# Attention in a decoder layer: denominators from products with ones, transposed heads side by side in one bank, their copies on ScalarE

## What is computed

```python
q = (x @ Wq).reshape(B, T, H, Dh)      # B=4, T=512, H=16, Dh=32; k and v likewise
scores = jnp.einsum('bthd,bshd->bhts', q, k)
scores = scores * jnp.tril(jnp.ones((T, T)))
attn = jax.nn.softmax(scores / T ** 0.5, axis=-1)
out = jnp.einsum('bhts,bshd->bthd', attn, v).reshape(B, T, H * Dh)
return out @ Wo
```

## Time and profile before

| | us |
|---|---|
| median of 3 runs (lowest, highest) | 1652.87 (1651.56, 1653.89) |
| profiled execution: span, first to last instruction | 1654.5 |
| PE / DVE / ACT / Pool busy in the span | 1527.9 / 1068.2 / 709.6 / 123.1 |
| attention loops, as read here | 90-161, 238-310, 389-461, 537-605 |

### The profile page before, as it was taken

How to read it: one execution, slowest core, us unless ns; L and a number is a source line. 1 busy time by engine, 2 the same in 40 slices (tenths; PEclk the granted TensorE clock), 3 DMA queues, 4 the chain that set the end, 5 groups by cost and what they waited for, 6 DMA issues and landing times.

```text
span 1654.5 us, 29864 instructions
## 1 busy us (share of the span) xinstructions
PE 1527.9 (92%) x9280; PEld 769.2 (46%) x9280; DVE 1068.2 (65%) x2408; ACT 709.6 (43%) x1578; POOL 123.1 (7%) x189
## 2 busy tenths in 40 slices
PE   5877987997799788989999999999999999999998
PEld 3455445545554554434444444444444444444443
DVE  6488568567955976666666666666666666666444
ACT  4378158526923862333333333333333333333332
POOL 1512002100300351000000000000000000000000
PEclk8999989998999999999999999999999999999999
DMA  6641432142125230211111111111111111111111
GB/s 191 160 144 51 121 91 72 53 127 89 59 78 149 84 97 23 80 40 67 53 40 65 54 40 64 55 40 61 58 40 58 60 40 57 62 40 42 59 51 51
DMA packets 73553, 118.41 MB, mean 72 GB/s; under 512 B 10096, under 2 KB 54384, under 8 KB 68848
## 3 DMA queue, kind: packets, MB, share of 16 engines
q1 hardware_dynamic: 73456, 117.20, 22.4%
HBM read 93.32 MB, written 23.86 MB: 71 GB/s over the span
## 4 chain that ended last, share of the span: by engine, by line
PE 78%; DVE 10%; issue 5%; SPq 2%; ACT 2%; DMA 2%; DVEq 0%; ACTq 0%
PE bank L538 23%; PE bank L539 23%; PE bank L540 23%; DVE bank L1144 3%; PE bank L595 3%; PE bank L614 2%; PE bank L551 1%; PE bank L584 1%; DVE mx L1144 1%; DMA qk_dram<-qk 1%; DVE w_split L1345 1%; PE bank L623 1%; DVE prob_t L1158 1%; PE bank L668 1%; PE bank L654 1%
## 5 line engine op out<-in xcount | busy, mean ns | idle before, releaser
L538 PE MATMUL bank<-xf,ring 128*128 128x512 f16 x1024 | 388.2, 379 | 0.0
L540 PE MATMUL bank<-xf,ring 128*128 128x512 f16 x1024 | 388.2, 379 | 0.0
L539 PE MATMUL bank<-xf,ring 128*128 128x512 f16 x1024 | 388.2, 379 | 0.0
L538 PE MATMUL bank<-ring,hid 128*128 (+1 forms) x512 | 195.5, 382 | 9.5 <-DVE hid L1277 6.4
L539 PE MATMUL bank<-ring,hid 128*128 (+1 forms) x512 | 195.6, 382 | 0.0
L540 PE MATMUL bank<-ring,hid 128*128 (+1 forms) x512 | 195.3, 381 | 0.0
L1270 DVE SCALAR_TENSOR_TENSOR cube<-sq,g_sb 128x512 f32<-128x512 f32 x128 | 88.4, 690 | 144.5 <-ACT sq L967 144.2
L1144 DVE CUSTOM_DVE_ANT_0 bank<-bank,mask,col 128x128 f32<-128x128 f32 (+3 forms) x256 | 142.3, 556 | 36.9 <-PE bank L584 23.2
L595 PE MATMUL bank<-ident,prob 128*128 128x128 f32 x640 | 121.4, 297 | 46.0 <-DVE prob_t L1158 39.3
L973 ACT CAST hid<-inter 128x512 f16<-128x512 f32 x128 | 79.0, 618 | 197.7 <-DVE inter L1275 197.7
L964 ACT ACTIVATE g_sb<-bank,col 128x512 f32<-128x512 f32 x128 | 87.7, 685 | 172.0 <-PE bank L540 172.0
(11 more groups left out here) (144 smaller groups left out, 2120.6 us busy)
## 6 DMA issues: line engine op xcount, KB each, us to landing
xf<-xf_dram SPq DMA_DIRECT2D x32, 1024.0 KB, 4.9
stack<-qk_dram SPq DMA_DIRECT2D x128, 128.0 KB, 3.2
sc_in<-scale_t SPq DMA_DIRECT2D x32, 384.0 KB
qk_dram<-qk SPq DMA_DIRECT2D x32, 256.0 KB, 3.1
packed_t<-pk_t SPq DMA_DIRECT2D x32, 192.0 KB, 2.0
pk_in<-packed_t SPq DMA_DIRECT2D x32, 192.0 KB
X<-in_x_dram SPq DMA_DIRECT2D x4, 1024.0 KB, 6.6
pk_in<-L_ffn_gate_W_packed_dram SPq DMA_DIRECT2D x16, 256.0 KB, 3.0
```

The costliest lines, as they stand in the source:

```text
L538: pe.matmul(o, lhs(0), rhs(0), start=first, stop=False)
L539: pe.matmul(o, lhs(0), rhs(1), start=False, stop=False)
L540: return pe.matmul(o, lhs(1), rhs(0), start=False, stop=stop)
```

## The change

On PE `values` first forms the denominators: for each block and head a product of `ones_col` (128 x 32 of ones) with prob_t into columns 256 and up of bank 6, and for i < 3 one more of `e_count` with the identity. `recips` is gone, and with it its slot and ACT's copy. Pool makes e_count = (512 - wide) e_zero. DVE's `divide` becomes a reciprocal of 128 x 128 from the bank, a wait for it, and the multiplication; it stands at j = 1 of unit u+3 (`AT_DIVIDE` 13). DVE's `turned`, `all_tokens` and `reciprocals` are gone, and ACT's `exp` has no accumulator. The transposes of several heads share a slot (`PACKED`: 4 heads at i = 0, 2 at i = 1, 1 else), and ACT copies each slot once. `repack` goes from j = 1 to j = 3, behind values; its copies move to i = 1, j = 1 on ACT and to i = 2, j = 0 on DVE.

```diff
-        def turn_slot(h):
-            return h + 2 * (max(0, h - 2) // 16) + max(0, h // 4 - 1)
+        PACKED = [TT // (i + 1) if i < 2 else 1 for i in range(TT)]
+        order = []
+        for u in range(UNITS):
+            for j in range(4):
+                if j % PACKED[u % TT] == 0:
+                    order.append(("heads", u, j // PACKED[u % TT]))
+                if j == 3 and u % TT == 0 and u > 0:
+                    order += [("pack", u // TT - 1, 0), ("pack", u // TT - 1, 1)]
+        order += [("pack", HG - 1, 0), ("pack", HG - 1, 1)]
...
-        AT_RECIP, AT_DIVIDE = 9, 12
-        AT_SUMS, AT_TURNED, AT_RECIPROCALS = 1, 3, 2
+        AT_DIVIDE = 13
...
+                nc.gpsimd.tensor_scalar(e_count[:, u % 2, :], e_zero[:, u % 2, :], float(T - wide[i]), None, ALU.mult).then_inc(e_count_done, 1)
...
             def values(n, u):
-                pe.wait_ge(pt_act, n * 3 * UNITS + 3 * u + 3)
-                pe.wait_ge(pt_dve, n * UNITS + u + 1)
+                pe.wait_ge(pt_out, n * TURNED + groups_till(u + 1))
                 if u >= 1:
                     pe.wait_ge(o_done, n * UNITS + u)
...
+                for k in range(blocks):
+                    for j in range(4):
+                        mm = pe.matmul(bank[6][32 * j:32 * j + 32, 256 + at:256 + at + P], ones_col[:], prob_t[:, u % 2, j, P * k:P * k + P],
+                                       start=(k == 0), stop=(k == blocks - 1 and i == TT - 1))
+                if i < TT - 1:
+                    pe.wait_ge(e_count_done, beyond_units(n, u))
+                    for j in range(4):
+                        mm = pe.matmul(bank[6][32 * j:32 * j + 32, 256 + at:256 + at + P], e_count[:, u % 2, j:j + 1].to_broadcast([P, DH]), ident[:],
+                                       start=False, stop=True)
...
                         if j == 3 and u > 0:
-                            recips(n, u - 1)
                             values(n, u - 1)
-                        if j == 1 and u % TT == 0 and u > 0:
+                        if j == 3 and u % TT == 0 and u > 0:
                             repack(n, u // TT - 1)
...
-                                     bias=nmx[:, u % 2, j:j + 1], accum_out=den[:, u % 2, j:j + 1]).then_inc(exp_done, 1)
+                                     bias=nmx[:, u % 2, j:j + 1]).then_inc(exp_done, 1)
...
             def turned(n, u, j):
                 i = u % TT
+                if j % PACKED[i] < PACKED[i] - 1:
+                    return
...
-                nc.scalar.copy(prob_t[:, u % 2, j, 0:wide[i]], turn_bank(turn_slot(4 * u + j))[:, 0:wide[i]]).then_inc(pt_act, 1)
+                heads = slice(j - PACKED[i] + 1, j + 1)
+                nc.scalar.copy(prob_t[:, u % 2, heads, 0:wide[i]],
+                               turn_bank(turn_slot(u, j))[:, 0:PACKED[i] * wide[i]].rearrange("p (j t) -> p j t", j=PACKED[i])).then_inc(pt_out, 1)
...
                         if j >= 2:
                             turned(n, u, j - 2)
-                        elif j == 0 and u > 0:
-                            turned(n, u - 1, 2)
-                        if j == 3 and u % TT == 0 and u > 0:
+                        elif u > 0:
+                            turned(n, u - 1, j + 2)
+                        if j == 1 and u % TT == 1 and u > TT:
                             repacked(n, u // TT - 1)
...
             def divide(n, u):
...
-                dve.wait_ge(rden_out, n * UNITS + u + 1)
                 dve.wait_ge(av_done, n * UNITS + u + 1)
+                nc.vector.reciprocal(r_den[:, u % 2, :], bank[6][:, 256 + P * (u % 2):256 + P * (u % 2) + P]).then_inc(rden_done, 1)
+                dve.wait_ge(rden_done, n * UNITS + u + 1)
                 nc.vector.scalar_tensor_tensor(o_sum[:, P * i:P * i + P], bank[6][:, P * (u % 2):P * (u % 2) + P], QS, r_den[:, u % 2, :],
                                                ALU.mult, ALU.mult).then_inc(o_done, 1)
```

More of the change, by code:

```diff
@@ L239, in decoder_layer, with groups_of, groups_till, turn_slot @@
         wide = [(i + 1) * P for i in range(TT)]
-        def turn_slot(h):
-            return h + 2 * (max(0, h - 2) // 16) + max(0, h // 4 - 1)
+        PACKED = [TT // (i + 1) if i < 2 else 1 for i in range(TT)]
+        def groups_of(u):
+            return TT // PACKED[u % TT]
+        def groups_till(u):
+            return sum(groups_of(v) for v in range(u))
+        TURNED = groups_till(UNITS)
+        order = []
[6 more added lines that the diff above has]
+        order += [("pack", HG - 1, 0), ("pack", HG - 1, 1)]
+        def turn_slot(u, j):
+            return order.index(("heads", u, j // PACKED[u % TT]))
         def pack_slot(r, half):
-            return (turn_slot(16 * r + 17) + 1 if r < HG - 1 else recip_slot(UNITS - 2) + 1) + half
-        def recip_slot(u):
-            return turn_slot(4 * u + 7) + 1 if u < UNITS - 1 else pack_slot(HG - 1, 1) + 1
+            return order.index(("pack", r, half))
         def turn_bank(slot):
@@ L255, in turn_read @@
         def turn_read(n, slot):
[L257 to L264, removed]
+            what, which, part = order[slot]
+            if what == "heads":
+                return pt_out, n * TURNED + groups_till(which) + part + 1
+            return (pk_out0, pk_out1)[part], n * (NB // B) + which + 1
         AHEAD = 3
-        AT_RECIP, AT_DIVIDE = 9, 12
-        AT_SUMS, AT_TURNED, AT_RECIPROCALS = 1, 3, 2
+        AT_DIVIDE = 13
         AT_OUT = 0
@@ L587, in turn @@
             def turn(n, u, j):
-                i, slot = u % TT, turn_slot(4 * u + j)
+                i, slot = u % TT, turn_slot(u, j)
+                at = wide[i] * (j % PACKED[i])
                 pe.wait_ge(exp_done, n * ROWS + 4 * u + j + 1)
[L590 to L593, removed]
+                if j % PACKED[i] == 0:
+                    if slot < 3:
+                        pe.wait_ge(att_lo, n * KT + (1, 2, 4)[slot])
+                    else:
+                        pe.wait_ge(*turn_read(n, slot - 3))
                 for k in range(wide[i] // P):
-                    mm = pe.transpose(turn_bank(slot)[:, P * k:P * k + P], prob[:, u % 2, j, P * k:P * k + P], ident[:])
+                    mm = pe.transpose(turn_bank(slot)[:, at + P * k:at + P * k + P], prob[:, u % 2, j, P * k:P * k + P], ident[:])
                 mm.then_inc(t_full, 1)
@@ L615, in values @@
                 mm.then_inc(av_done, 1)
[L617 to L622, removed]
-                    mm = pe.matmul(turn_bank(slot)[32 * j:32 * j + 32, 0:P], r_col[:, u % 2, j:j + 1].to_broadcast([P, DH]), ident[:], start=True, stop=True)
-                mm.then_inc(r_full, 1)
             def out_proj(n):
@@ L813, in between @@
                     value_sum(n + 1, 2)
[L815 removed]
+            pe.wait_ge(const_done, 4)
             pe.wait_ge(ld_s, 48)
@@ L1392, in body @@
                             row_max(n, u, j)
-                        if j == AT_SUMS and u > 0:
-                            all_tokens(n, u - 1)
-                        if j == AT_TURNED and u > 0:
-                            turned(n, u - 1)
-                        if j == AT_RECIPROCALS and u > 0:
-                            reciprocals(n, u - 1)
                         h = 4 * u + j - AT_DIVIDE
@@ L1404, in body @@
                             shift(n, u, j)
-                        if j == 0 and u % TT == 1 and u > TT:
+                        if j == 0 and u % TT == 2 and u > TT:
                             repacked(n, u // TT - 1)
```

50 lines of the change are left out of this document (7 added, 43 removed).

## The result

The changed kernel took 1715.41 us (median of 4 runs, 1712.39 to 1716.05) against 1653.38 before (1651.56 to 1654.36): ratio 1.0373, 95% interval 1.0356 to 1.0389, 3.7% slower. Now and then an execution of one and the same program comes out some 3% longer at a lower granted clock (once among those of the kernel before, 1704.85 us at 0.93); no ratio here counts one. The forecast was 1709 in a range of 1663 to 1728. The span of the profiled execution grew from 1654.5 to 1714.3, by 59.8 us; the forecast said 56.6.

The account below looks back on a forecast made before the run. The prediction took DVE's in-order list to set the pace, with PE late at two places. Its terms, +11.8 + 26.6 + 25.8 - 4.4 - 3.9 + 0.7 = +56.6 us on 1652.87, gave 1709, range 1663 to 1728.

Parts of the forecast that it names:

- A: DVE's stretch from second 128-column row to first 256-column row, twelve times: 37.2 us before, 49.0 forecast, +11.8.
- B: DVE's stretch from second 256-column row to first 384-column row, twelve times: 32.5 us before, 59.2 forecast, +26.6.
- the tails: From a loop's last row onward: -3.9 us over three loops, and +0.7 for the last loop's final divide.
- DVE's in-order list sets the pace: In the attention loops PE's idle time costs nothing as long as DVE starts its next row on time.
- ACT: Accumulator reads and copies removed on ACT priced at 0; rival that ACT becomes the bound: 1727 us, chance 0.07.
- Reciprocal of 128 x 128: DVE's widened reciprocal in the divide: taken as 1.0 us, with 0.30 and 1.25 kept as ends.
- d: Length of DVE's 128x128 reciprocal, taken as 1.0 us; each 0.1 us of it is 5.2 us over 52 divides.
- half clock: PE at half clock in the first of the two tight places: up to 4.2 us, adding 2 us each time.
- 28 other divisions: Seven divides per loop in 384- and 512-column rows, each d - 0.08 longer: 28 x 0.92, +25.8 us.
- Removed DVE work: DVE's copies, sums and small reciprocals taken away, mostly hidden already: -4.4 us.
- The rival that PE's waits were on the path: PE's 46.0 us of waiting before its transposes come back: 1639 us, or 1654 with a third left; chance 0.09.

Follow-up runs that it names:

- four products: The changed kernel with its denominators replaced by four products of ones_col with the identity, every denominator then 1: 1695.67 us, ratio 1.0236 to the kernel before.
- accumulator: The changed kernel with the exponentials' sums taken on ACT as before, their result used by nobody: 1709.74 us, ratio 1.0334 to the kernel before.

## Why the prediction was right, and where it was off

The mechanism came as forecast: the reciprocal's length at every division, and PE late at A and B. That the sum came within 3.2 us of the span's growth (56.6 against 59.8) is in part luck. B cost 8.4 us more than its term and the tails 2.4 more, while the other rows cost 5.0 less and the first row began 2.3 earlier.

1. *DVE's in-order list sets the pace, PE's place in it matters at A and B only.* Right as to the added products, which show in the rows of A and B and, beside them, only in the tail of a loop (four products), and as to ACT, where 52 us more cost nothing (accumulator). "DVE hardly ever stands waiting for PE inside a loop" holds but for A. The page before has the row maxima with

```profile
L1144 DVE CUSTOM_DVE_ANT_0 bank<-bank,mask,col 128x128 f32<-128x128 f32 (+3 forms) x256 | 142.3, 556 | 36.9 <-PE bank L584 23.2
```

   and of these 23.2 us for PE's scores 18.8 stand in the first unit of each sequence and 4.4 in places A.
2. *Reciprocal of 128 x 128.* 0.954 us for a forecast of 1.0 between 0.30 and 1.25. The further columns cost 6.3 ns each; the estimate that came nearest was the one of 6 ns from the two 128x4 rows. The Trainium skill ("VectorE: DVE Perf Modes", the walkthrough) has a repeat count of 8; read as eight engine clocks for each element, that is an estimate of 1.07, 12% high. The slope of six times a multiplication's fits a reciprocal that takes several passes; no run here shows how it is made.
3. *Place A.* 3.08 + d is 4.03 with the measured d; the loops show 3.97 to 4.25, the last sequence 4.06. The sum of the twelve is right to 1% (48.7 against 49.0).
4. *Place B.* 3.93 + d is 4.88 against 4.83. The term fell short by 8.4 us, on what it left out: the half clock at six of the twelve (4 x 1.61, 1.25 and 1.61: 9.3). The prediction had priced a half clock only at A and left it out of the sum. No B has it without the repack behind the values, nor with the division a row earlier, nor with the cheap operation for the reciprocal, which leaves both orders as they are; with the accumulator's reads on ACT three B have it, with four products six. So the order on PE alone does not decide it.
5. *28 other divisions.* d - 0.08 is 0.87; a 512-column row takes 1.93 with the division and 1.10 without, 0.83. *Removed DVE work* was put at 4.4. These rows as a whole came out 5.0 us lower than forecast. The shorter reciprocal is 28 x 0.046 = 1.3 of it. 1.9 are a move that the sum left out, DVE's copy of the repack's second half. Before, it stood in the first 256-column row, behind a wait for PE's transposes; in the changed kernel it stands in the first 384-column row, without one:

```profile
426.26 0.56 DVE L1198 CAST pk_t<-bank 128x768 int16<-128x768 f16 x1 [0.35 <-PE bank L688]
...
444.40 0.56 DVE L1174 CAST pk_t<-bank 128x768 int16<-128x768 f16 x1
```

   The twelve steps from there to the second 256-column row lost 6.6 us, and the twelve from the first to the second 384-column row became 4.7 longer. Another 1.0 is the idle stretch ("issue") in the third head group that is gone (three steps of 1.44, now 1.09); it was no wait for PE, and its cause is open. The last 0.8 was not traced.
6. *The rival that PE's waits were on the path.* Not the case as priced (46 us, or a third of it), but not empty: taking the copies off DVE is worth 10 to 12 us, most of it by PE's release. The prediction had read the 39.3 us of PE's waiting as free. Three of the places A at 4.20, 4.20 and 3.62 us, 3.8 us in all, went with the copies. Ahead of each of the three PE had just stood waiting for such a copy, 1.50, 1.51 and 2.28 us; the first:

```profile
253.51 0.66 PE L595 MATMUL bank<-ident,prob 128*128 128x128 f32 x4 [1.50 <-DVE prob_t L1158]
```

   That the copies caused them is likely and not shown: a wait of 2.28 us that ended at 439.11 was followed by a place A at full clock.
7. *The tail* gave 2.0 us of the 3.9.

## What to carry to other kernels

An operation's price on an in-order engine is its length only where nothing already hides it; its place in the list decides how much of another engine's list stands behind it. Before a division is widened from 4 columns to 128, its slope by column is the number to get: here six times that of a multiplication. And a change with several parts is worth taking apart: its copies on ACT alone make the kernel before 0.6 to 0.7% faster (1644 us), while the whole change, with them in it, costs 3.7%.

## What was not expected of the hardware

The half clock. In the kernel before it stands at three of twelve places A (granted clock 0.61, 0.72 and 0.66 over the place), once of twelve with the division at 13, and at none of 48 (all 1.00) in the four profiles of that kernel in which the copies are on ACT. In the changed kernel it left A and came to six B. Each count is that of one profile. All these stand right behind a wait of PE for DVE, with a dense group of products to do; but PE's 2.0 us of idle time precede the B at full clock as well (440.46 and 483.32 above), so the wait alone does not tell them apart. What does is open. One costs 1.3 to 1.6 us at B and 0.6 to 1.6 at A.
